# Routing of second halves moved into the expert tile loops of a four-layer gated transformer kernel

## The reference

```python
x = x + jnp.tanh(g_xattn[0]) * _L0_xattn_ref(_layernorm(x), ctx_768, ...)   # 16 heads of 8
x = x + jnp.tanh(g_ffn[0])   * _L0_ffn_ref(_layernorm(x), ...)              # 8 experts, top 2, gelu
x = x + jnp.tanh(g_xattn[1]) * _L1_xattn_ref(_layernorm(x), ctx_768, ...)   # 16 heads of 64
x = x + jnp.tanh(g_ffn[1])   * _L1_ffn_ref(_layernorm(x), ...)              # 8 linear experts, mixed
x = x + jnp.tanh(g_xattn[2]) * _L2_xattn_ref(_layernorm(x), ctx_768, ...)   # one head of 128
x = x + jnp.tanh(g_ffn[2])   * _L2_ffn_ref(_layernorm(x), ...)              # 8 experts, top 1, silu
x = x + jnp.tanh(g_xattn[3]) * _L3_xattn_ref(_layernorm(x), ctx_768, ...)   # 16 heads of 8
x = x + jnp.tanh(g_ffn[3])   * _L3_ffn_ref(_layernorm(x), ...)              # ternary weights
```

## Time and profile before

| | us |
|---|---|
| median of 3 runs | 796.48 (789.18 to 797.4) |
| profiled execution, its own time | 798.17 |
| its span, first to last instruction | 796.1 |
| busy in the span: TensorE, VectorE, ScalarE, GpSimd | 668.2, 453.5, 395.7, 311.3 |

### The profile page before, as it was taken

One profiled execution on the slowest core, in us unless ns is written; L12 is line 12 of the kernel. 1 busy time (PEld: TensorE's weight loads), 2 busy tenths in 40 slices (PEclk: granted clock), 3 DMA queues, 4 the chain that ended last, 5 costly groups with the idle time before them and its releaser, 6 DMA issues.

```text
span 796.1 us, 17394 instructions
## 1 busy us (share of the span) xinstructions
PE 668.2 (84%) x6461; PEld 561.5 (71%) x6461; DVE 453.5 (57%) x1407; ACT 395.7 (50%) x969; POOL 311.3 (39%) x266
## 2 busy tenths in 40 slices
PE   3698994489999797999999999795699967997885
PEld 2487783379899786888886854564489856776774
DVE  4366868523234568475666767655533346778752
ACT  3466541146555465365555567321155846665641
POOL 4555532726052256122232337401324457454131
PEclk9999998589999899799999999985599989999977
DMA  5543651766863201000000020002447643620001
GB/s 146 146 117 92 195 179 57 235 188 188 250 185 113 73 21 27 1 1 2 1 2 0 2 80 1 1 1 69 134 138 228 178 134 91 159 68 2 3 13 40
DMA packets 60716, 70.92 MB, mean 89 GB/s; under 512 B 7051, under 2 KB 40859, under 8 KB 60635
## 3 DMA queue, kind: packets, MB, share of 16 engines
q1 hardware_dynamic: 57563, 63.52, 28.4%
q0 software_dynamic: 3072, 6.30, 2.6%
HBM read 48.89 MB, written 20.91 MB: 88 GB/s over the span
## 4 chain that ended last, share of the span: by engine, by line
PE 65%; DVE 15%; POOL 5%; ACT 5%; DMA 4%; issue 4%; SPq 0%; POOLq 0%; ACTq 0%; DVEq 0%
PE banks L1435 8%; PE banks L1451 7%; PE banks L1550 5%; PE banks L1252 4%; PE banks L1559 4%; PE banks L1570 4%; PE banks L1164 3%; PE banks L1275 3%; PE banks L1122 3%; PE banks L1264 3%; PE banks L1123 3%; PE banks L1124 3%; PE banks L1603 2%; DMA xsb<-xs 2%; PE banks L1230 2%
## 5 line engine op out<-in xcount | busy, mean ns | idle before, releaser
L961 ACT ACTIVATE hT<-banks,wup 128x128 f32<-128x128 f32 x304 | 86.5, 369 | 72.0 <-PE banks L1435 71.1
L892 ACT ACTIVATE pT<-banks 77x512 f32<-77x512 f32 x128 | 69.0, 589 | 49.2 <-PE banks L1252 48.6
L605 POOL TENSOR_TENSOR kbd<-k,const 96x1248 fp32r<-96x1248 f32 x32 | 72.7, 2284 | 36.2 <-PE banks L1252 33.7
L700 POOL DMA_INDIRECT xs<-xn,slot x48 | 46.9, 977 | 101.1 <-DVE ysb L2205 50.4
L1435 PE MATMUL banks<-xTs,wup 128*128 128x128 f32 x608 | 83.6, 283 | 2.0 <-ACT hT L961 1.2
L660 POOL TENSOR_TENSOR sh<-sh,rd 128x616 f32<-128x616 f32 x32 | 38.9, 1217 | 115.0 <-DVE rd L1850 115.0
L1451 PE MATMUL banks<-wd,hT 128*128 x608 | 80.4, 276 | 0.1
L1435 PEld LDWEIGHTS banks<-xTs,wup 128*128 128x128 f32 x608 | 77.4, 200 | 2.7 <-issue 2.4
L1451 PEld LDWEIGHTS banks<-wd,hT 128*128 128x128 f32 x608 | 73.7, 192 | 0.4 <-issue 0.3
L2205 DVE COPY ysb<-banks 128x128 f32<-128x128 f32 x76 | 22.1, 291 | 90.3 <-PE banks L1451 89.1
L585 POOL TENSOR_TENSOR rstd<-vv,const 128x4 f32<-128x4 f32 x24 | 25.4, 1059 | 111.2 <-DVE vv L1801 110.9
(11 more groups left out here) (322 smaller groups left out, 1595.8 us busy)
## 6 DMA issues: line engine op xcount, KB each, us to landing
wup<-in_up SPq DMA_DIRECT2D x76, 258.0 KB, 3.4
q<-queries SPq DMA_DIRECT2D x21, 256.0 KB, 4.2
queries<-qc SPq DMA_DIRECT2D x8, 512.0 KB
wd<-in_down SPq DMA_DIRECT2D x8, 512.0 KB, 6.1
ys<-ysb SPq DMA_DIRECT2D x16, 256.0 KB
k<-keys SPq DMA_DIRECT2D x24, 156.0 KB, 3.7
xs<-zt SPq DMA_DIRECT2D x2, 1472.0 KB, 10.6
keys<-kc SPq DMA_DIRECT2D x8, 312.0 KB, 4.3
```

The costliest lines, as they stand in the source:

```text
L605: pool.tensor_tensor(kbd[b % NB8][0:96, :, :, :].bitcast(F32R), kb, m, ALU.mult).then_inc(h8.kbd, 1)
L700: pool.indirect_dma_start(xs[hh], bass.IndirectOffsetOnAxis(ap=idx[hh % 2][k_][:, t:t + 1], axis=0), xn8[hh % 2][:, t, :], None).then_inc( ...
L892: act.activation(pT[b % 2][0:SK, u, :], ps[0:SK, 2 + u % 2, :], ACT.Exp, scale=D8 ** -0.5)\
L961: ins = act.activation(hT[T % 3][:, c, :], ps[:, T % 2, c * P:c * P + P], func, bias=wup[T % NW][:, HID + c:HID + c + 1])
```

## The change

Half 0's work moves to earlier places of the attention steps, on TensorE and ScalarE into the middle of a step. In `experts` the choice, ranks and slots of half 1 and half 3, their tanh, and their bias work move to named tiles of the loop of the first half. In run 0 the logits of half 1 move behind the first three slot turns. Logits and ranks get banks of their own. `token_roots` of the next half moves from scatter 3 to scatter 9 in half 0 (it stays at 3 in half 2), and `length_roots(1)` behind all of half 0's scatters. The first line of the loop in `down` only says which tile waits for the tile list.

```diff
+        def logits_bank(hh):
+            return (7, 3, 0, 3)[hh]
+        def ranks_bank(hh):
+            return (7, 2, 1, 2)[hh]
...
 # GpSimd, spread(hh)
-                        if hh % 2 == 0 and m == 3:
+                        if m == (9 if hh == 0 else 3) and hh % 2 == 0:
                             token_roots(hh + 1)
-                        if hh == 0 and m == 6:
-                            length_roots(1)
...
+                if hh == 0:
+                    length_roots(1)
...
 # ScalarE, heads8: step b
                         query_hi(run, g + 1)
+                    if run == 0 and b in (11, 12):
+                        turned(0, b - 11)
                     exps(b, (2, 3))
...
-                    if run == 0 and b in (11, 12):
-                        turned(0, b - 11)
...
 # ScalarE, experts
-                tanh(2 * run + 1)
...
                         hidden(BASE[hh] + i)
+                        if h == 0 and i == (7, 4)[run]:
+                            tanh(hh + 1)
...
 # TensorE, heads8: step b
                         project(b - 2)
+                    if run == 0 and b == 11:
+                        turn(0, 0)
+                    if run == 0 and b == 12:
+                        logits(0)
+                    if run == 0 and b == 15:
+                        ranks(0)
                     if b + 1 < B:
                         scores(b + 1, 1)
...
-                    if run == 0 and b in (11, 12):
-                        turn(0, b - 11)
-                    if run == 0 and b == 13:
-                        logits(0)
-                    if run == 0 and b == B:
-                        ranks(0)
+                    if run == 0 and b == 11:
+                        turn(0, 1)
...
 # TensorE, logits(hh) and ranks(hh)
+                if hh % 2:
+                    pe.wait_ge(mo.xb, 2 * hh)
...
-                bank = routed(hh)[1]
+                bank = ranks_bank(hh)
...
 # TensorE, down(T)
-                    if j < 2:
-                        pe.wait_ge(mo.tiles, 2 * run + j + 1)
+                    if j % nt == 0:
+                        pe.wait_ge(mo.tiles, 2 * run + j // nt + 1)
...
 # TensorE, experts
                 turn(hh + 1, 1)
-                logits(hh + 1)
-                ranks(hh + 1)
+                if run:
+                    logits(hh + 1)
                 for i in range(3):
                     turn_slots(first + i)
+                if run == 0:
+                    logits(hh + 1)
                 for i in range(2):
                     up(first + i)
...
-                        if h == 0 and i == 2:
+                        if h == 0 and i == (5, 2)[run]:
+                            ranks(hh + 1)
+                        if h == 0 and i == (9, 6)[run]:
                             second_bias(hh + 1)
-                        if h == 0 and i == 4:
+                        if h == 0 and i == (12, 9)[run]:
                             add_bias(hh + 1)
...
 # VectorE, first_route(b), at the end of step b
-                if b in (10, 11):
-                    norm8(0, b - 10)
+                if b == 10:
+                    norm8(0, 0)
+                    norm8(0, 1)
+                if b == 12:
+                    route_top2(0, 0)
+                    route_top2(0, 1)
                 if b == 13:
-                    route_top2(0, 0)
+                    route_top2(0, 2)
                 if b == 14:
-                    route_top2(0, 1)
-                    route_top2(0, 2)
+                    route_top2(0, 3)
                 if b == 15:
-                    route_top2(0, 3)
-                if b == 16:
                     slots(0)
...
 # VectorE, experts
-                for part in range(4):
-                    route(hh + 1, part)
-                slots(hh + 1)
...
                         give(T + i, i)
                         if h == 0:
-                            if i == 0:
+                            if run == 0 and i < 4:
+                                route(hh + 1, i)
+                            if run and i == 0:
+                                route(hh + 1, 0)
+                                route(hh + 1, 2)
+                            if run and i == 1:
+                                route(hh + 1, 3)
+                            if i == (6, 3)[run]:
+                                slots(hh + 1)
+                            if i == (8, 5)[run]:
                                 weigh(hh + 1, gate)
-                            if i == 2:
+                            if i == (10, 7)[run]:
                                 bias8(hh + 1, 0)
-                            if i == 5:
+                            if i == (13, 10)[run]:
                                 bias8(hh + 1, 1)
```

More of the change, by code:

```diff
@@ L1381, in logits @@
                 pe.wait_ge(mo.w, run + 1)
+                if hh % 2:
+                    pe.wait_ge(mo.xb, 2 * hh)
                 for t in range(HT):
-                    ins = pe.matmul(ps[:, routed(hh)[0], t * 16:t * 16 + n_], xT8[:, t // GB, (t % GB) * P:(t % GB) * P + P],
+                    ins = pe.matmul(ps[:, logits_bank(hh), t * 16:t * 16 + n_], xT8[:, t // GB, (t % GB) * P:(t % GB) * P + P],
                                     rraw2[2 * run][:, 0:n_], start=True, stop=True)
@@ L2007, in route_top2 @@
                     dve.wait_ge(mo.r, hh + 1)
-                    o_ = ps[:, routed(hh)[0], 0:HT * 16].rearrange("p (t e) -> p t e", e=16)
+                    o_ = ps[:, logits_bank(hh), 0:HT * 16].rearrange("p (t e) -> p t e", e=16)
                     lk.mark(dve.tensor_copy(R[2], o_[:, :, 0:E]))
```

## The result

The changed kernel took 804.06 us (median of 4, 802.15 to 810.62) against 794.73 for the kernel before beside it: ratio 1.0122, 95% interval 1.0086 to 1.0159. It is slower, as forecast (806, range 790 to 813), and the interval lies clear of 1.

What follows compares the result with a forecast made beforehand. GpSimd's scatters were taken to bound the time before the first tile, TensorE the loop. Start +4.1, loop +4.9, late scatter +4.0 and run 1 -3.4 sum to +9.6 on 798.17 (807.8); less 1.7 above the median, 806 us, range 790 to 813.

Steps and rivals of the forecast that it cites:

- Two regimes: Ahead of the first tile GpSimd's sixteen scatters set the end; inside the tile loop TensorE does, busy 40.38 of 40.40 us.
- Attention, +2.4: Half 0's routing put into attention steps delays them by 6.3, so slots(0) starts 2.4 us later; bounds -3.9 to +4.
- Roots, -1.9: Length root leaves half 0's scatter chain: 1.67 and its pause, -1.9 us; token root moved to scatter 9 costs nothing.
- Logits, +3.6: Run 0: half 1's logits stand between arrival of the slots and first up, without speeding the ups: +3.6 us, bounds 1.8 to 3.6.
- Loop of half 0, +4.9: Half 1's choice and slots exceed the tile slack by 4.6, ranks add 0.3: +4.9 us, bounds 0.3 and 7.
- the slack of a tile: In the tile loops, VectorE work that fits between giving one tile and taking the next without delaying TensorE: 1.05 us.
- Late scatter, +4.0: Half 1's last scatter ends 4.3 late, 1.4 spare: +2.9; slow start +1.6, second load's 0.5 wait gone: +4.0, bounds 0 and 6.
- The slow start: Behind the 3.9 us wait for half 1's first slots the clock falls, costing 3.42 - 1.78 = +1.6 us.
- Run 1, -5.9 and +2.5: Choice, ranks and slots leave the path before run 1's ups, -5.9 us; its loop gives back +2.5; net -3.4.
- All hidden: Rival: VectorE's insertions in attention and loop cost nothing, slack 3.2 us a tile; -8.0, 788.5 us; chance 0.22.
- Absorbed: Rival: attention absorbs the routing (0, not 2.4) and the clock stays up at half 1's slots; +5.6, 802 us; chance 0.25.
- Tables: Rival: tanh in the loops needs its own ScalarE table, +4.1 us for both runs; +13.7, 810 us; chance 0.08.

Runs made afterwards that it cites:

- the first set: Follow-ups on chip 7, kernel before at 796.13 us: run 1's changes alone, attention's alone, split of value weights behind tile 0, logits ahead of the turns.
- the two variants of the whole change: Changed kernel with GpSimd's split of value weights behind tile 0, 1.0117 of before; changed kernel with half 1's logits ahead of the slot turns, 1.0123.
- the early split: Changed kernel with GpSimd's split of layer 1's value weights behind the first give instead of between scatters 7 and 8: 1.0117 of the kernel before.

## Why the prediction was right

- **Direction.** Two regimes, and the routing of the second half is worth moving only where it stands on the path. In the first set, without a hole, run 1's changes alone are at 0.9968 and attention's alone at 1.0052, against 1.012 for the two variants of the whole change beside them: by difference about 1% is left for run 0's loop, logits and roots, as their stretches add up to (+8.2 expected). The direct test, run 0's loop alone, was measured only in sets with holes (1.0175 and 1.0181, with one of 9.1 and one of 9.2), so its ratio holds more than the edits.
- **Size, in part luck.** The forecast sum was +9.6, the medians differ by 9.3. But the stretches that the forecast priced add up to 6.1 in the pair of traces, and to 7.9 with the mean of seven traces for attention. The loop of half 0 and the late scatter were priced 2.4 too high together; the 1.4 between 7.9 and 9.3 is put down to no term, and is less than two executions of one kernel differ by (802.15 to 810.62).
- **Attention, +2.4.** The profiled execution gave +1.0, and is the lowest of the seven traces with these edits: they took 41.88 to 45.09 from root to scatter, 43.70 in the mean, against 40.87 in the mean of six without them. So +2.8, near the forecast, but not by its terms: the maximum was late where said, at 1.61 (115.10) rather than 2.4, and TensorE's waits in this stretch (those over 0.15 us) add up to 6.6 to 7.2 us instead of 5.1, 1.5 to 2.1 more. The rest goes with the clock, where the prediction had let one fall cancel another. Over the stretch the granted clock was 0.96 in the three traces that took 41.9 to 42.8, 0.92 in the one of 43.4 and 0.89 in the three of 45.1, all with much the same waits; without the edits it was 0.94. It falls at different places: it read 0.66 at 100 to 105 before and 1.00 after; in the kernel with attention's changes alone it read 0.60 at 114 to 122.
- **Roots, -1.9.** -1.8, one root's time. The prediction did not say that the token root, left at scatter 3, would wait 1.26 for VectorE.
- **Logits, +3.6.** +3.4; last scatter to first up is 9.3 to 9.9 in the six traces with the logits behind the turns, 6.0 to 6.3 in the eight without. That the 3.4 reach the end of the kernel is not shown.
- **Loop of half 0, +4.9.** +4.1. The mis-sized term is the slack of a tile. Behind part 1, part 3 and slots TensorE's waits are 0.17, 1.16 and 1.72 against 0.5, 1.6 and 2.1, each 0.3 to 0.4 less, so the slack is about 1.4 rather than 1.05. They make 3.05 of the 4.1; the other 1.0 is in steps of 2.1 to 2.3 behind ranks (priced at 0.3) and behind the two larger waits, which the prediction did not price.
- **Late scatter, +4.0.** +2.4. Last scatter 4.48 behind tile 15 (forecast 4.9). SP's load left 7.57 behind that tile's copy where it had left 4.21, so 3.4 later and not 2.9; but it took 3.09 instead of 4.32, which no term foresaw, and so the wait was 3.11 instead of 3.9. The slow start was 0.86 for the up and 0.4 for the down, instead of 1.6. In the sets with holes the scatter catches up in the hole and the wait goes: the last scatter was 0.57 behind tile 15 there.
- **Run 1, -5.9 and +2.5.** -5.6 and +2.5, with waits of TensorE of 1.49 behind slots, 0.29 behind part 3 and 0.61 behind weigh. From half 2's root to the first up took 37.7 to 40.2 in the ten traces with these edits, 43.6 to 44.5 in the four without.
- **Rivals.** All hidden: out by TensorE's three waits. Absorbed: its clock half is out (1.92 for the up), and so is its attention half, by the mean of +2.8; the first trace alone, +1.0, would not have told. Tables: out, all fourteen traces have six table loads, as before, and none stands beside a tanh in the loops.
- **What was not in it.** The forecast had no term for rows of back-to-back scatters. Between the two traces of the kernel after, gives 0 to 15 take 7.6 us more and run 1's gives 4.3 more, of which gives 15 to 45 give 2.3 back: that is 9.5 of the 9.6 between the two spans. That the change is at 1.018 in some sets was not foreseen. Among the expectations, the one for the early split priced the split by its time on GpSimd alone; beside a choice on VectorE it cost TensorE 2.49 more.

## What to carry to other kernels

Work moved into a loop that is bound by one engine is paid for beyond the slack of each period, here about 1.4 us in a period of 1.9; moving it gains only where it stood on the path, as in run 1. When a producer moves, look at the queue that waits on it: its requests now come late and in a burst. Look also at what the fixed work in that queue then stands beside: GpSimd's split beside VectorE's choice stopped both VectorE and TensorE, and beside VectorE's copies it stopped nothing. A loop must be measured in more than one set, on more than one chip, before a hole in it is put down to an edit.

## What was not expected of the hardware

- The holes: 3.0 to 9.6 us between two gives in which VectorE and ScalarE stand, in both sets where the kernel before takes 800, in neither measurement where it takes 795 to 796. In the long ones (5.8 and more) no record names what releases one engine or both. That they come with scatters issued back to back is a correlation over sixteen loops; a kernel that spaces the scatters out was not tried. TensorE's records in a hole don't fit ScalarE's (in the last fence the down product at 590.92 stands ahead of the silu that it reads, which is in the group at 592.87), so the cause can't be read from the trace and stays open.
- The same attention code took from 41.88 to 45.09 us in seven traces, three of them 45.06 to 45.09; their granted clock was 0.89 where the fastest three had 0.96.
- A VectorE operation of 0.22 us lasted 2.20 beside one of GpSimd of 2.34.
